# Moving the first load of x from ScalarE's DMA queue to SyncE's, between the constants and w1, in a conditioned two-layer kernel

## The reference, cut to what matters

```
h     = silu(noise_encoding(t) @ W1 + b1) @ W2 + b2       # 16 samples, 512 features
scale = h @ Wsc + bsc ;  shift = h @ Wsh + bsh             # 256 each, per sample
y   = silu(scale * layer_norm(x, gamma, beta) + shift) @ W_in + b_in
out = silu(scale * layer_norm(y, gamma, beta) + shift) @ W_out + b_out + x
```

## Time and profile before

| what | value |
|---|---|
| runs of the kernel before | 82.94, 82.47, 82.25 us; median 82.47 |
| span of the profiled execution | 80.7 us |
| PE busy | 75.0 us, 93% of the span |
| DVE busy | 61.3 us, 76% |
| ACT busy | 55.8 us, 69% |
| POOL busy | 53.3 us, 66% |
| read from memory, written | 7.65 MB, 4.19 MB |
| chain that ended last, by engine | POOL 41%, PE 27%, issue 25%, DVE 2% |

### The profile page before, as it was taken

The page is one execution under the profiler, slowest core; times in us unless marked ns, Lnnn a source line. Parts: engine busy times, 40 slices in busy tenths (PEclk is TensorE's granted clock), DMA queues, the critical chain, the costliest instruction groups (busy, mean ns, idle before and its releaser), DMA issues.

```text
span 80.7 us, 1314 instructions
## 1 busy us (share of the span) xinstructions
PE 75.0 (93%) x293; PEld 37.2 (46%) x293; DVE 61.3 (76%) x181; ACT 55.8 (69%) x174; POOL 53.3 (66%) x63
## 2 busy tenths in 40 slices
PE   4999899999989999999999899999999899999950
PEld 1367547468633444444453443444454344445420
DVE  1085797879899979999879868886194697989560
ACT  4202410999939998977999997799936998967000
POOL 4000283999999999999999999999999303020000
PEclk9999999999999999999999999999999999999999
DMA  1799999999500000201130033030307200030835
GB/s 8 279 446 398 426 384 400 406 410 404 238 8 4 0 0 0 103 27 64 70 127 3 0 130 132 6 134 0 130 4 282 108 0 0 0 129 1 325 141 184
DMA packets 4903, 11.92 MB, mean 148 GB/s; under 512 B 672, under 2 KB 928, under 8 KB 4768
## 3 DMA queue, kind: packets, MB, share of 16 engines
q1 hardware_dynamic: 4752, 11.33, 36.7%
q10 hardware_dynamic: 144, 0.52, 1.6%
HBM read 7.65 MB, written 4.19 MB: 147 GB/s over the span
## 4 chain that ended last, share of the span: by engine, by line
POOL 41%; PE 27%; issue 25%; DVE 2%; POOLq 0%; ACT 0%; ACTq 0%
POOL act L326 16%; POOL act L331 11%; PE acc L978 11%; POOL act L320 7%; PE acc L849 6%; POOL rstd L304 5%; PE acc L954 5%; PE acc L989 2%; POOL rstd L314 1%; PE acc L852 1%; PE acc L999 1%; DVE o_sb L716 1%; PE stat_m L1007 1%; PE stat L898 0%; DVE spread L621 0%
## 5 line engine op out<-in xcount | busy, mean ns | idle before, releaser
L426 ACT ACTIVATE act<-act,cond 128x256 f32<-128x256 f32 x64 | 35.9, 594 | 5.6 <-POOL act L331 3.6
L978 PE MATMUL acc<-act,wout_sb 128*128 128x512 f32 x60 | 27.5, 600 | 0.0
L954 PE MATMUL acc<-act,win_sb 128*128 128x512 f32 x56 | 26.9, 608 | 0.5 <-ACT act L426 0.2
L331 POOL TENSOR_TENSOR act<-act,beta_sb 128x512 f32<-128x512 f32 x13 | 16.5, 1281 | 0.7
L326 POOL TENSOR_TENSOR act<-act,gamma_sb 128x512 f32<-128x512 f32 x13 | 16.6, 1284 | 0.3
L978 PEld LDWEIGHTS acc<-act,wout_sb 128*128 128x128 f32 x60 | 10.9, 189 | 12.4 <-issue 9.0
L446 ACT ACTIVATE squares<-acc,shift 128x256 bf16<-128x256 f32 x32 | 14.7, 464 | 2.1 <-PE acc L954 1.3
L704 DVE SCALAR_TENSOR_TENSOR act<-acc,shift,gamma_sb 128x256 f32<-128x256 f32 x32 | 14.3, 476 | 1.4 <-ACT squares L446 1.3
L954 PEld LDWEIGHTS acc<-act,win_sb 128*128 128x128 f32 x56 | 9.8, 190 | 10.5 <-issue 7.5
L711 DVE SCALAR_TENSOR_TENSOR act<-act,rstd,beta_ps 128x512 f32<-128x512 f32 x16 | 11.6, 742 | 3.4 <-issue 2.5
L716 DVE SCALAR_TENSOR_TENSOR o_sb<-acc,const_sb,x_sb 128x512 f32<-128x512 f32 (+1 forms) x17 | 11.9, 713 | 2.4 <-PE acc L978 2.3
(11 more groups left out here) (74 smaller groups left out, 53.7 us busy)
## 6 DMA issues: line engine op xcount, KB each, us to landing
out_dram<-o_sb SPq DMA_DIRECT2D x15, 256.0 KB, 2.0
x_sb<-x_dram SPq DMA_DIRECT2D x7, 512.0 KB, 12.8
w_sb<-w_dram SPq DMA_DIRECT2D x1, 1024.0 KB, 6.2
wss_sb<-wss_dram SPq DMA_DIRECT2D x1, 768.0 KB, 8.5
x_sb<-x_dram ACTq DMA_DIRECT2D x1, 512.0 KB, 3.9
w_sb<-w_dram SPq DMA_DIRECT2D x1, 256.0 KB, 4.1
gamma_sb<-gamma_dram SPq DMA_DIRECT2D x1, 256.0 KB, 6.4
wss_sb<-wss_dram SPq DMA_DIRECT2D x1, 256.0 KB, 8.7
```

What stands on the lines that cost most here:

```text
L331: nc.gpsimd.tensor_tensor(act1[:, p, :, b], act1[:, p, :, b], beta_sb[:], ALU.add).then_inc(z1_pool, 1)
L426: return nc.scalar.activation(buf[:, c, b], buf[:, c, b], ACT.Silu, bias=cond[:, 1, c, i:i + 1], scale=cond[:, 0, c, i:i + 1], **kw)
L954: mm = nc.tensor.matmul(y_slot(p, c)[:].rearrange("p b s -> p (b s)"), win_sb[:, k, c * P:(c + 1) * P], act1[:, p, k].rearrange("p b s -> ...
L978: mm = nc.tensor.matmul(bank_of(("O", p, c, 0, BP))[:].rearrange("p b s -> p (b s)"), wout_sb[:, k, c * P:(c + 1) * P], act2[:, p, k].rear ...
```

## The change

The load of x of pair 0 is no longer ACT's first instruction. It is SP's second, behind the constants and ahead of w1. All of SP's later issues keep their order and stand one place further back. ACT's program begins with the table load. No wait, no buffer and no arithmetic is changed.

```diff
@@ block.sync @@
             sp.dma_start(const_sb[:], consts).then_inc(const_in, 16)
+            load_x(0)
             sp.dma_start(w1_sb[:], w1).then_inc(w1_in, 16)
             sp.dma_start(w2_sb[:], w2).then_inc(w2_in, 16)
             sp.dma_start(gamma_sb[:], gamma).then_inc(gamma_in, 16)
@@ block.scalar @@
-            act.dma_start(x_sb[:, 0], x[0]).then_inc(x_in[0], 16)
             nc.scalar.preload_act_table_set("silu_and_others")
```

## The result

| | before | changed |
|---|---|---|
| runs with the change as it stands | 82.36 us (82.02 to 82.94, 4 runs) | 84.08 us (83.56 to 84.74, 4 runs) |
| ratio, 95% interval | | 1.0201 (1.0133 to 1.0268) |
| second series (experiment `again`) | 82.27 us (29 runs) | 83.70 us (82.52 to 84.62, 12 runs) |
| ratio, 95% interval | | 1.0116 (1.0075 to 1.0157) |
| span of the profiled execution | 80.7 | 81.8, in a run of 83.56 us |

The change makes the kernel slower by 1.2 to 2%, where 82.45 was forecast, in a range of 81.95 to 82.95. The ratios leave out runs that lie over 1.5% above a kernel's fastest, which takes out five of the twelve runs of `again` and five of the twelve of `one_block` further down, so for these two the medians (1.017 and 1.009) say more than the ratio. The scatter is itself part of the result: 2.1 us in `again` against 1 us before.

The account below looks back on a forecast made before the run. PE's warm matmuls pace the start, POOL carries the middle, PE's own work bounds the end. All terms 0, at most 0.1 us of mean gain: 80.7 + 1.8 - 0.05 = 82.45 us, range 81.95 to 82.95.

Parts of the forecast that it names:

- Everything behind it: Loads from w1 on: same bytes ahead, DMA engines full from 2.6 us, so only the start's loss shifts them; cost 0.
- D: Shift of the whole load stream by what is lost at the start: 0 to 0.33 us, 0.44 at most, taken 0.1.
- Rival B: Slow DMA start-up comes again between constants and pair 0: shift 1.44, cost 0.9 us, time 83.4; chance 0.05 in full.
- second slow second: The low-rate DMA second from 1.6 to 2.6 us (23 GB/s), supposed to come again behind pair 0's issue.
- The cost formula: At pair 1's statistics on DVE: cost max(0, D - 0.55), so 0 for 0.1 and for 0.44.
- the cover: Slack for a late pair 1: 0.07 us before DVE starts on it plus 0.48 of DVE's idleness at 12.63.
- The constants: First load, alone at the start: land at 3.4 us instead of 4.1, DVE's encoding ends about 0.7 earlier; worth 0.
- ACT, and pair 0 on PE's side: ACT's table load about 0.4 us earlier, worth 0; pair 0 lands at 4.8, needed by 6.6, worth 0.
- The cap at the end: Before 63.41 us PE hardly idles, so an earlier POOL gives back at most 0.2 to 0.5 us.
- The rule on issuing engines: Moving the load to SP gives away one issue, 0.44 us; changes the landings and still costs 0 at the end.

Follow-up runs that it names:

- again: The changed kernel once more, nothing edited; 83.70 us, ratio 1.0116.
- one_block: Changed kernel with the constants and w1 joined in one load, so that w2 is issued at 1.62; 82.98 us, ratio 1.0037.
- x0_after_table: Kernel before with ACT's first two instructions exchanged, table load then pair 0, which was still issued beside the table load; 82.09 us, ratio 0.9980.
- w2_late: Kernel before with SP held ahead of w2 by an extra POOL memset, w2 issued at 2.02, no load added; 82.77 us, ratio 1.0052.
- w1_act: Changed kernel with w1 loaded as ACT's first instruction instead of on SP, w2 issued at 1.62; 82.62 us, ratio 1.0040.
- gamma_act: Changed kernel with gamma loaded as ACT's first instruction instead of on SP; 82.38 us, ratio 0.9999.
- const_act: Changed kernel with the constants loaded as ACT's first instruction instead of on SP; 82.77 us, ratio 1.0062.
- spare_act: Changed kernel plus a second, unread copy of the constants loaded as ACT's first instruction; 83.53 us, ratio 1.0122.
- table_late: Changed kernel with ACT's table load held back by a wait for POOL's second memset; 83.79 us, ratio 1.0153.
- hold: Changed kernel with SP waiting for pair 0 to land before it issues wss and all behind it; 83.77 us, ratio 1.0207.
- w2_halves: Changed kernel with w2 loaded by two DMAs of 512 KB with 4 KB rows; 83.79 us, ratio 1.0220.
- wss_one: Changed kernel with the two loads of wss made one load of 1024 KB, all on SP; 84.34 us, ratio 1.0215.

## Why the prediction was wrong

**The step that failed** is "Everything behind it": that the whole stream shifts only by what is lost at the start, D = 0 to 0.44, since the same bytes are ahead of it and the engines are full from 2.6 us on. The start lost almost nothing, as said: pair 0 landed at 4.7 (taken: 4.8), w1 at 5.4. But the stream was not full at 5 us. At the first rows of w2 some DMA engines stood (for 0.6 to 2.2 us in the slow profiles), and w2, gamma and pair 1 came 1.7 to 1.8 us later. I had read the rate as a property of the bytes; in the kernel before it was a property of when each load was issued, too. The range of D came from the length of an issue and of the start-up; no row of before bounded a stall in the middle.

**Rival B was nearest in effect.** It had D = 1.44, cost 0.9, 83.4; measured were 1.7 at pair 1 and 0.98 at POOL. Its mechanism was wrong: there was no second slow second behind the issue, and the stall came 2.5 us later. It had 0.05, because I argued from the start alone.

**The cost formula held, nearly.** max(0, D - 0.55) gives 1.15 for D = 1.7; POOL's power moved by 0.98. Line 605 of pair 1 started 1.66 us later (11.50 in place of 9.84), so the cover was 0.68. That the loss passes through DVE's stats of pair 1 was right. That pair 1's landing is what holds them was half of it: the prediction gave gamma a lateness of under 0.1 us for D up to 0.44, but gamma had no slack before its copy, and at D = 1.7 that copy held DVE until 10.90. By the estimate above this alone brings line 605 to 11.3, against 11.5 as measured.

**The constants** were mis-sized, without harm: taken 3.4 and bounded by 3.2, landed at 2.5. They flow before the full rate of 2.6 when nothing is beside them. The trace shows the other case as well: beside pair 0 they took 3.4 us to land, alone 1.8. The Trainium skill, DMA: Bandwidth & Descriptors, section "Queues, rings and completion order", has each DMA engine alternate packet by packet between the queues that have work; by that rule the small packets of the constants wait for the large ones of pair 0, and the trace agrees: alone, the 128 packets of the constants start between 1.71 and 2.15 us; beside pair 0 the last starts at 3.56, with pair 0's packets (0.16 us each) in between.

**ACT, and pair 0 on PE's side**, went as said: 0. The earlier constants gained nothing by themselves, and pair 0 had its 1.0 us of cover before line 617.

**The cap at the end was wrong**, and it did not matter here. I had read 0.2 us of waiting before 63.41 as the most that an earlier POOL could give back. In x0_after_table POOL's second power came at 13.22, 0.77 us before that of the earlier trace rows, and the span was 80.0, 0.7 less; span minus power is the same 66.6 to 67.1 everywhere. PE's waits from 24 us on are 0.3 + 0.2 us in x0_after_table too, as in the earlier trace rows: they were not used up, so all of PE's work behind that point moved with POOL. A small wait at one place was no measure of what an earlier start can give.

**The rule on issuing engines**, in the section "Issuing engines are not separate DMA queues" of the Trainium skill's DMA: Bandwidth & Descriptors, has a second issuing engine save only the issue time, and calls that usually small. By that, with 0.44 us given away and the formula above, the change would have cost nothing at the end. That it costs nothing these runs don't bear out: 0.4 us of issue time was worth 1.1 us of landing in w2_late.

**What stays open** is why the engines stop at w2's rows. Shown: it hangs on when w2 is issued (w2_late; one_block and w1_act, with half of the loss or more gone, agree), and not on that alone (gamma_act, with w2 issued at 2.09, is free of it in its times). It hangs on what else is queued at the start, too (const_act and gamma_act are free of it; spare_act, table_late, hold are not), but by which rule is not shown. Ruled out as the cause: chance alone, the number of loads outstanding, the table load, the mere lack of a second queue, packets of the instruction queues, and, for the time though not for the long packets, 8 KB rows. There is one more pattern that I can't order into cause and effect: in eight of the nine profiles with w2 in at 8.9 us or later (all but w2_halves) one SP issue between 4 and 6 us takes 0.9 to 1.4 us, and it begins up to 1.1 us ahead of the slow packets of w2 or, in hold and wss_one, 0.4 behind the first of them. In before it takes at most 0.71.

## What to carry to other kernels

The time of an issue is part of a load's price even where the load won't flow for 3 us: a DMA put ahead of others in a queue should be costed with a late and uneven landing of all behind it, not with its bytes and 0.4 us alone. Compare the landing of each load with the start of its first user: here pair 1 had 0.07 us and gamma none, and through these two the loss came. When a launch scatters more after a change, take a second trace before explaining the first; one of the two traces of the changed kernel had next to no stall in it.

## What the runs showed of the hardware

- A load is in when the last of its 16 increments is; in the changed kernel two slow shares out of 16 held up the landing of nine loads in a row, w2 to pair 3, by 1.2 to 1.5 us, and did not catch up in between.
- In the kernel before, a packet of 16 KB on the queue "q8 instruction" took 1.07 us from 15.44, and one share of each of the next six loads landed 1.4 to 1.5 us behind the others. All profiles have such a packet.
- 0.4 us of later issue made 1.1 us of later landing (one profile of w2_late).
- 50.5 KB alone land 1.8 us after the issue, beside a 512 KB load 3.4.
- ACT issues a DMA at 0.74 us while its table load runs from 0.71 to 1.99 (x0_after_table).
- PE's start scatters by its clock: the eight warm matmuls took 3.60 us before and 3.29 in the changed kernel's profile, the three after them 1.03 and 0.67. Each time PE had worked without a stop since 1.17 us; the column of the granted clock reads 1.00 in both.
